# A relational graph network on one core: broadcast multiplies at the end, another order of transfers and other second norms at the start

## The chip, the core and the metric

The kernel runs on one core of a Trainium2 chip. Its engines are TensorE (PE), VectorE (DVE), ScalarE (ACT), GpSimd (POOL) and SyncE (SP), each with its own program; transfers issued by SP, ACT and POOL are moved by 16 DMA engines. The metric is the device time of one launch in microseconds (us).

## The reference

128 graphs of 128 nodes with 128 features, x; integers adj, 128x128 for each graph. With the drawn inputs adj is 0 or 1, and the code for other integers (`general`) is not entered.

```
h    = x @ W_loop.T                          # [128 graphs, 128 nodes, 128]
g    = h @ Wg_loop.T
v    = (h + b_loop) * sigmoid(g + bg_loop)
s    = x + relu(adj.T @ v)                   # first sum
x1   = (s - mean(s)) / sqrt(var(s) + 1e-5)   # first norm, over the features
m    = adj @ x1                              # messages
z    = x1 + m @ W1 + bias                    # second sum
out  = (z - mean(z)) / sqrt(var(z) + 1e-5)   # second norm
```

## The kernel before

The graphs go in 32 groups of four (GB = 4, W = 512 columns), q = 0 to 31. The host lays x, x transposed, adj and adj transposed out by group; adj and adj_t come in pairs of groups, 512 KB each. The mean of z is taken out ahead: VectorE centres the message weight and the bias (`message_weight`, `message_weight_end`, with one TensorE product L596 between), so that the second norm is only a multiply of z by 1/sqrt(var).

Each engine has a loop over t, and works on several groups with lags. TensorE at t: `loop_sum(t-1)`, `project(t)`, `message_weights(t-3)`, `messages(t-2)`; up to t = 4 (FILL) the projection comes before the loop sum, and y and messages run one group later until t = 6 (CAUGHT_UP). `project(q)` makes h and g in PSUM on top of biases that ScalarE copied there (`seed(q)`, at t = q - 2, once values(q - 2) are out). ScalarE: `copy_messages`, `norm2(t-6)` for graphs 0 and 1, `gates(t)`, `norm2` for graphs 2 and 3, `look` (counts odd integers), `seed(t+2)`. In groups 0 to 3 it also makes half of x1 (`shared_norm1`).

VectorE: `first_sum` (L930), two `bn_stats` (`first_stats`), `first_moments` (variance and mean, 128x4 each), `values(t)` (L920), `second_sum` (L990), `second_stats`. Between them it runs a chain of nine operations on 128x4 (`inverse_root`), one chain for each group from q = 0 on (FIRST_CHAIN = 5 is the t of the first), to get 1/sqrt of the second variance. `norm2(q)` waits for the chain's end.

GpSimd: for each group `norm1`: a power on 128x4 (L378), a product (L381), four multiply-adds to x1 (L387); then the issue of the next adj or adj_t transfer (L361, L368).

At the head SP issues in the order wg, w_loop_t, xt 0, raw (the integers of group 0, 256 KB, cast to floats by VectorE at L835), xt 1, x 0, xt 2, x 1, constants (192 KB), xt 3, x 2, xt 4, x 3. GpSimd issues the integers of group 1 (L415), waits for raw, issues the pair of groups 2 and 3 (`load_adj(1)`) and the transposed pair 0 and 1 (`load_adjt(0)`), waits for xt 2, issues `load_adj(2)`, and enters its loop.

At the tail the last five groups (27 = LAST to 31) get 1/sqrt from GpSimd (`last_variance` on VectorE, `last_power` on GpSimd, L409), group 31 in two halves (`half_variance2`, `half_power`, L404). Groups 30 and 31 have x1 added inside PSUM by TensorE (`inject`). ScalarE makes norm2 of 27, 28 and 30, VectorE of 29 and 31 (`last_norm2`, one multiply L1014 for each graph).

Of the kernel before, what the change touches and what calls it, by code (L numbers as in the profile page):

```python
# [47 lines left out]
FIRST_CHAIN = STAT2_LAG  # L48
# [29 lines left out]
def build(nc, x, x_t, adj, adj_t, w_in, w_loop_t, wg_loop_t, gate_bias, consts,  # L78
          w_rel_t, wg_rel_t, b_rel, bg_rel, w_msgs, rel_ids, out):
    with ExitStack() as ctx:  # L80
# [33 lines left out]
        power = sb("power", [P, GB], F32)  # L114

# [51 lines left out]
        first_adj = sem("first_adj")  # L167
        consts_in = sem("consts_in")
# [20 lines left out]
        last_power_done = sem("last_power_done")  # L189
        mean_done = sem("mean_done")  # L190
# [97 lines left out]
        def _(sp):  # L288
# [15 lines left out]
            load_xt(0)  # L304

            sp.dma_start(raw[:, :], adj[0, :, 0:W]).then_inc(raw_in, 16)  # L306
            load_xt(1)
            load_x(0)
            load_xt(2)
            load_x(1)  # L310
            sp.dma_start(const_sb[:, :], consts).then_inc(consts_in, 16)
            load_xt(3)
# [10 lines left out]
            store(LAST)  # L323
            sp.wait_ge(out_done, LAST + 2)
            store(LAST + 1)
            sp.wait_ge(out_dve, 2)
            store(LAST + 2)
            sp.wait_ge(out_done, LAST + 3)
            store(LAST + 3)
            sp.wait_ge(out_dve, 4)  # L330
# [24 lines left out]
        def _(pool):  # L355
# [50 lines left out]

            def last_power(q):
# [9 lines left out]
            pool.wait_ge(raw_in, 16)  # L417
            load_adj(1)
            load_adjt(0)
            pool.wait_ge(xt_in[2], 16)  # L420
            load_adj(2)
            pool.wait_ge(power_ready, 1)
            for t in range(GROUPS + NORM1_LAG):
# [4 lines left out]
                if t % 2 == 1:  # L428
                    load_adjt(t // 2 + 1)
                elif t > 0:  # L430
                    load_adj(t // 2 + 2)
            half_root1(0)
# [17 lines left out]
        def _(pe):  # L450
# [25 lines left out]
            def loop_sum(q):  # L476
                if exists(q):
                    spot = q // 2 % ADJ_RING * 2 + q % 2
                    if q == 0:
                        pe.wait_ge(first_adj, 1)  # L480
                    else:
# [57 lines left out]
            def messages(q):  # L539
                if exists(q):  # L540
                    spot = q // 2 % ADJ_RING * 2 + q % 2
                    pe.wait_ge(adjt_in[q // 2 % ADJ_RING], arrived(q // 2, ADJ_RING))
# [66 lines left out]
            half_messages(0)  # L609
            half_messages(1)  # L610
            half_inject(0)
# [47 lines left out]
        def _(act):  # L659
# [42 lines left out]
            def norm2(q, graphs):  # L702
                if exists(q):
                    t = q + STAT2_LAG
                    if q < LAST:
# [5 lines left out]
                    for b in graphs:  # L711
                        c = (q - LAST) * GB + b
                        r = rstd2[:, t % RSTD_RING, b:b + 1] if q < LAST else last_rstd[:, c:c + 1]
# [17 lines left out]
            def look(q):  # L731
                if exists(q):
                    spot = q // 2 % ADJ_RING
                    if q == 0:
                        act.wait_ge(first_adj, 1)
                    else:
                        act.wait_ge(adj_in[spot], arrived(q // 2, ADJ_RING))
# [81 lines left out]
        def _(dve):  # L819
# [78 lines left out]

            def last_variance(q):
# [107 lines left out]
            def last_norm2(q, graphs):  # L1007
# [3 lines left out]
                for b in graphs:  # L1011
                    c = (q - LAST) * GB + b
                    z = y_of(q, b, 1) if q in INJECTED else z_sb[:, q % Z_RING, batch(b)]
                    last = ts(out_sb[:, q % OUT_RING, batch(b)], z, last_rstd[:, c:c + 1], None, ALU.mult)  # L1014
                last.then_inc(out_dve, 1)
# [206 lines left out]
```

## Time and profile before

| what | value |
|---|---|
| median of 3 runs | 158.72 us (158.67 to 159.06) |
| the profiled execution's own time | 159.4 us |
| its span in the profile | 157.3 us |
| TensorE matmul busy | 148.7 us (95%) |
| VectorE busy | 138.4 us (88%) |
| ScalarE busy | 128.2 us (81%) |
| GpSimd busy | 113.5 us (72%) |
| moved by DMA | 42.74 MB, mean 272 GB/s |

The span is the stretch that the profile covers; the time around it (2.1 us here) is launch and end. Busy times of TensorE are modelled, since matmuls overlap. In the rows, "[idle before <-X]" is how long an engine stood and what released it; PEld is TensorE's weight load; an engine name with q is its instruction queue.

### The profile page before, as it was taken

How to read it: one execution, taken by the hardware profiler on the slowest of the kernel's cores; microseconds unless marked ns; L12 is line 12 of the kernel's file. 1: busy time of each engine (PE TensorE's matmuls, PEld its weight loads, DVE VectorE, ACT ScalarE, POOL GpSimd, SP SyncE). 2: the span in 40 equal slices, each digit the busy share in tenths (PEclk: the TensorE clock that was granted, in tenths of full speed). 3: DMA queues.
4: the chain of work that ended last, by engine and by line, in shares of the span. 5: the costliest groups of instructions: out<-in, count | busy, mean ns of one | idle time of the engine just before them, and what ended most of it. 6: DMA issues, size and time to landing. Idle time of an engine off the chain costs nothing.

```text
span 157.3 us, 3862 instructions
## 1 busy us (share of the span) xinstructions
PE 148.7 (95%) x1055; PEld 138.5 (88%) x1055; DVE 138.4 (88%) x567; ACT 128.2 (81%) x293; POOL 113.5 (72%) x221
## 2 busy tenths in 40 slices
PE   6789999999999999999999999999999999999950
PEld 3478998999999999999999999999999999999940
DVE  1329979799999999999999999999999999999962
ACT  3557997788788888998888888998888888978960
POOL 1314988865877877887777887887777886876770
PEclk9999999999999999999999999999999999999996
DMA  4899999987799899999999999998989854151144
GB/s 125 291 395 398 399 400 400 374 301 213 251 305 297 291 293 301 302 304 304 265 313 288 306 298 305 311 285 293 324 279 308 251 190 163 67 200 71 64 179 168
DMA packets 19319, 42.74 MB, mean 272 GB/s; under 512 B 2144, under 2 KB 2784, under 8 KB 19296
## 3 DMA queue, kind: packets, MB, share of 16 engines
q1 hardware_dynamic: 14400, 25.76, 48.5%
q0 software_dynamic: 4608, 16.52, 32.9%
q8 instruction: 9, 0.15, 0.4%
q10 hardware_dynamic: 288, 0.20, 0.4%
q14 instruction: 14, 0.11, 0.2%
HBM read 34.08 MB, written 8.39 MB: 270 GB/s over the span
## 4 chain that ended last, share of the span: by engine, by line
PE 84%; DVE 4%; DMA 4%; issue 3%; POOL 2%; SPq 1%; POOLq 0%; DVEq 0%
PE hg_ps L472 33%; PE loop_ps L487 18%; PE y_ps L576 16%; PE msg_ps L552 16%; DMA xt_sb<-x_t_dram 4%; POOL last_rstd L409 1%; DVE last_stats L1003 1%; POOL last_rstd L404 1%; PE aux_ps L552 1%; DVE x L973 1%; DVE s_sb L947 0%; DVE out_sb L1014 0%; DVE z_sb L990 0%; DVE stats L935 0%; SPq L306 0%
## 5 line engine op out<-in xcount | busy, mean ns | idle before, releaser
L472 PE MATMUL hg_ps<-w_all,xt_sb 128*128 128x256 f32 x256 | 60.8, 380 | 1.4 <-DMA xt_sb<-x_t_dram 1.4
L472 PEld LDWEIGHTS hg_ps<-w_all,xt_sb 128*128 128x128 f32 x256 | 46.2, 190 | 7.3 <-DMA xt_sb<-x_t_dram 1.8
L387 POOL TENSOR_SCALAR x<-s_sb,rstd,nmr 128x128 f32<-128x128 f32 x114 | 49.7, 448 | 3.3
L378 POOL TENSOR_TENSOR rstd<-var,power 128x4 f32<-128x4 f32 x31 | 32.0, 1033 | 21.0 <-DVE var L912 18.3
L715 ACT ACTIVATE out_sb<-z_sb,rstd 128x128 f32<-128x128 f32 x108 | 36.9, 392 | 0.5 <-DVE rstd L884 0.5
L673 ACT ACTIVATE hg_ps<-gate_b 128x1024 f32<-128x1024 f32 (+1 forms) x32 | 31.9, 1000 | 2.9 <-DVE vals L920 2.1
L682 ACT ACTIVATE gate<-hg_ps 128x512 f32<-128x512 f32 x32 | 19.1, 596 | 18.0 <-PE hg_ps L472 17.8
L487 PE MATMUL loop_ps<-vals,adj_sb 128*128 128x128 f32 x248 | 33.0, 276 | 0.2
L576 PEld LDWEIGHTS y_ps<-w,msg_t 128*128 128x128 f32 x240 | 31.3, 191 | 1.5
L576 PE MATMUL y_ps<-w,msg_t 128*128 128x128 f32 x240 | 31.8, 275 | 0.0
L487 PEld LDWEIGHTS loop_ps<-vals,adj_sb 128*128 128x128 f32 x248 | 30.4, 192 | 0.8 <-issue 0.5
L552 PE MATMUL msg_ps<-adjt_sb,x 128*128 128x128 f32 x232 | 30.6, 275 | 0.0
L552 PEld LDWEIGHTS msg_ps<-adjt_sb,x 128*128 128x128 f32 x232 | 28.2, 192 | 0.0
L930 DVE SCALAR_TENSOR_TENSOR s_sb<-loop_ps,x_sb 128x512 f32<-128x512 f32 x31 | 21.3, 689 | 7.3 <-PE loop_ps L487 4.0
L935 DVE BATCH_NORM_STATS2 stats<-s_sb 128x6 f32<-128x256 f32 x62 | 25.5, 427 | 0.0
L1003 DVE BATCH_NORM_STATS2 stats<-z_sb 128x6 f32<-128x256 f32 x54 | 22.8, 426 | 0.0
L740 ACT ACTIVATE seen<-adj_sb,half 128x512 bf16<-128x512 f32 x32 | 22.7, 709 | 0.0
L920 DVE TENSOR_TENSOR vals<-hg_ps,gate 128x512 f32<-128x512 f32 x32 | 21.7, 679 | 0.9 <-ACT gate L682 0.8
L990 DVE TENSOR_TENSOR z_sb<-y_ps,x 128x512 f32<-128x512 f32 x30 | 20.4, 679 | 1.1 <-PE y_ps L576 1.1
L692 ACT ACTIVATE msg_t<-msg_ps 128x512 f32<-128x512 f32 x29 | 16.8, 579 | 0.0
L361 POOL DMA_DIRECT2D adj_sb<-adj_dram x15 | 9.3, 623 | 5.5 <-DMA xt_sb<-x_t_dram 2.9
L368 POOL DMA_DIRECT2D adjt_sb<-adj_t_dram x16 | 10.1, 631 | 0.0
(93 smaller groups left out, 119.2 us busy)
## 6 DMA issues: line engine op xcount, KB each, us to landing
xt_sb<-x_t_dram SPq DMA_DIRECT2D x32, 256.0 KB, 4.3
x_sb<-x_dram SPq DMA_DIRECT2D x32, 256.0 KB, 4.3
adjt_sb<-adj_t_dram POOLq DMA_DIRECT2D x16, 512.0 KB, 4.9
out<-out_sb SPq DMA_DIRECT2D x32, 256.0 KB, 3.3
adj_sb<-adj_dram POOLq DMA_DIRECT2D x15, 512.0 KB, 5.2
raw<-adj_dram SPq DMA_DIRECT2D x1, 256.0 KB, 4.3
adj_sb<-adj_dram POOLq DMA_DIRECT2D x1, 256.0 KB, 6.6
const_sb<-consts_dram SPq DMA_DIRECT2D x1, 192.0 KB, 7.1
```

Source lines behind the costliest of these rows:

```text
L378: nc.gpsimd.tensor_tensor(r, var1[:, q % 2, :], power[:, :], ALU.pow).then_inc(rstd1_done, 1)
L387: done = nc.gpsimd.tensor_scalar(x1[:, q % X1_RING, batch(b)], s_sb[:, q % S_RING, batch(b)], r[:, b:b + 1], n[:, b:b + 1], ALU.mult, ALU.add)
L472: last = nc.tensor.matmul(hg_ps[:, q % 2, b, :], xt_sb[:, q % XT_RING, batch(b)], w_gate, start=False, stop=True, skip_group_check=True)
L487: last = nc.tensor.matmul(loop_ps[:, batch(b)], adj_sb[:, spot, batch(b)], vals[:, q % 2, batch(b)], start=True, stop=True)
L552: last = nc.tensor.matmul(msg_of(q)[:, batch(b)], x1[:, q % X1_RING, batch(b)], adjt_sb[:, spot, batch(b)], start=True, stop=True)
L576: last = nc.tensor.matmul(y_of(q, b, 1), msg_t[:, q % 2, batch(b)], w1[:, :], start=q not in INJECTED, stop=True, skip_group_check=q in IN ...
L673: nc.scalar.activation(hg_ps[:, q % 2, 0:graphs, :], gate_b[:, None, :].broadcast_to([P, graphs, 2 * P]), ACT.Copy).then_inc(seeded, 1)
L715: last = nc.scalar.activation(out_sb[:, q % OUT_RING, batch(b)], z, ACT.Copy, scale=r)
L740: nc.scalar.activation(seen[:, :], adj_sb[:, 2 * spot + q % 2, :], ACT.Square, bias=half[:, 0:1], accum_out=seen_sum[:, q:q + 1]).then_inc ...
L920: tt(vals[:, q % 2, :].rearrange("p (b n) -> p b n", b=GB), hg_ps[:, q % 2, :, 0:P], gate[:, q % 2, :].rearrange("p (b n) -> p b n", b=GB) ...
L935: got = nc.vector.bn_stats(stats[:, q % STATS_RING, p, :], s_sb[:, q % S_RING, 2 * p * P:2 * (p + 1) * P].rearrange("p (i n) -> p n i", i=2))
L1003: got = nc.vector.bn_stats(into, z.rearrange("p (i n) -> p n i", i=2))
```

## The change

- Head, SP: xt 1 goes ahead of raw, and xt 3 ahead of the constants.
- Head, GpSimd: it waits for xt 1 instead of raw, and issues the integers of groups 2 and 3 and the transposed ones of 0 and 1 as four transfers of 256 KB; group 2's and transposed group 0's have semaphores of their own. It waits for xt 3 instead of xt 2 ahead of `load_adj(2)`.
- The first half of the weight's steps on VectorE runs at t = 2 instead of t = 1.
- Second norms 0 and 1: no chains (FIRST_CHAIN = 7); VectorE writes the variance, GpSimd takes the power after norm1 and the issue of t = 5 and 6; ScalarE's norm2 waits for it.
- Tail, TensorE: half_inject(0) ahead of half_messages(1).
- Tail, VectorE: another order; half_norm1(1) after the statistics and variance of group 29; the variance of group 30 ahead of the norm of group 29; `last_norm2` is one tensor_tensor for all its graphs, with 1/sqrt as a broadcast operand: one of 128x512 from SBUF for group 29, two of 128x256 from PSUM for group 31.
- Tail, SP: store 29 ahead of store 28.

```
-FIRST_CHAIN = STAT2_LAG
+EARLY = 2
+FIRST_CHAIN = STAT2_LAG + EARLY
 ...                                                     # SP
             load_xt(0)
+            load_xt(1)
             sp.dma_start(raw[:, :], adj[0, :, 0:W]).then_inc(raw_in, 16)
-            load_xt(1)
             load_x(0)
             load_xt(2)
             load_x(1)
+            load_xt(3)
             sp.dma_start(const_sb[:, :], consts).then_inc(consts_in, 16)
-            load_xt(3)
...
             store(LAST)
+            sp.wait_ge(out_dve, 1)
+            store(LAST + 2)
             sp.wait_ge(out_done, LAST + 2)
             store(LAST + 1)
-            sp.wait_ge(out_dve, 2)
-            store(LAST + 2)
             sp.wait_ge(out_done, LAST + 3)
             store(LAST + 3)
-            sp.wait_ge(out_dve, 4)
+            sp.wait_ge(out_dve, 3)
             store(LAST + 4)
...
+            def early_power(q):
+                pool.wait_ge(early_var_done, q + 1)
+                nc.gpsimd.tensor_tensor(early_rstd[:, q, :], early_var[:, q, :], power[:, :], ALU.pow)\
+                    .then_inc(early_power_done, 1)
...
-            pool.wait_ge(raw_in, 16)
-            load_adj(1)
-            load_adjt(0)
-            pool.wait_ge(xt_in[2], 16)
+            pool.wait_ge(xt_in[1], 16)
+            pool.dma_start(adj_sb[:, 2, :], adj[1, :, 0:W]).then_inc(alone_adj, 16)
+            pool.dma_start(adjt_sb[:, 0, :], adj_t[0, :, 0:W]).then_inc(alone_adjt, 16)
+            pool.dma_start(adj_sb[:, 3, :], adj[1, :, W:2 * W]).then_inc(adj_in[1], 16)
+            pool.dma_start(adjt_sb[:, 1, :], adj_t[0, :, W:2 * W]).then_inc(adjt_in[0], 16)
+            pool.wait_ge(xt_in[3], 16)
             load_adj(2)
...
+                if 0 <= t - STAT2_LAG < EARLY:
+                    early_power(t - STAT2_LAG)
...
             half_messages(0)
+            half_inject(0)
             half_messages(1)
-            half_inject(0)
...
+                    if q < EARLY:
+                        act.wait_ge(early_power_done, q + 1)
-                    if q < LAST:
+                    elif q < LAST:
...
+            def early_variance(q):
+                dve.wait_ge(bn2_done, q + 1)
+                m2 = stats[:, q % STATS_RING, 2:4, :].rearrange("p c (i k) -> p (c i) k", k=3)[:, :, 2]
+                ts(early_var[:, q, :], m2, 1.0 / P, EPS, ALU.mult, ALU.add).then_inc(early_var_done, 1)
...
-                for b in graphs:
-                    c = (q - LAST) * GB + b
-                    z = y_of(q, b, 1) if q in INJECTED else z_sb[:, q % Z_RING, batch(b)]
-                    last = ts(out_sb[:, q % OUT_RING, batch(b)], z, last_rstd[:, c:c + 1], None, ALU.mult)
-                last.then_inc(out_dve, 1)
+                n, b = len(graphs), graphs[0]
+                c, columns = (q - LAST) * GB + b, slice(b * P, (b + n) * P)
+                z = y_of(q, b, n) if q in INJECTED else z_sb[:, q % Z_RING, columns]
+                tt(out_sb[:, q % OUT_RING, columns].rearrange("p (b n) -> p b n", b=n),
+                   z.rearrange("p (b n) -> p b n", b=n),
+                   last_rstd[:, c:c + n, None].broadcast_to([P, n, P]), ALU.mult).then_inc(out_dve, 1)
...
-                    next(steps)                             # t == CAUGHT_UP
...
-                if t == 1:
+                if t == 2:
                     weight_steps = message_weight()
                     next(weight_steps)
-                if t == 2:
                     next(weight_steps, None)
...
             half_norm1(0)
             second_stats(LAST + 2, 0)
-            half_norm1(1)
+            second_stats(LAST + 2, 1)
             dve.wait_ge(odd_count, 1)
             nc.vector.tensor_copy(flag[:, :], aux_ps[0:1, 2 * P:2 * P + 1]).then_inc(flag_ready, 1)
-            second_stats(LAST + 2, 1)
+            last_variance(LAST + 2)
+            half_norm1(1)
             second_stats(LAST + 3, 0)
-            last_variance(LAST + 2)
             second_stats(LAST + 3, 1)
-            last_norm2(LAST + 2, (0, 1))
             last_variance(LAST + 3)
+            last_norm2(LAST + 2, every)
             second_stats(LAST + 4, 0)
-            last_norm2(LAST + 2, (2, 3))
             half_variance2(0)
             second_stats(LAST + 4, 1)
```

## Rows read from the trace of the kernel before

**Rows 1.** The page: the chain's shares by engine, and GB/s in 40 slices.

```profile
GB/s 125 291 395 398 399 400 400 374 301 213 251 305 297 291 293 301 302 304 304 265 313 288 306 298 305 311 285 293 324 279 308 251 190 163 67 200 71 64 179 168
...
PE 84%; DVE 4%; DMA 4%; issue 3%; POOL 2%; SPq 1%; POOLq 0%; DVEq 0%
```

**Rows 2.** The chain of waits in order of time: start, duration, what.

```profile
2.72 5.71 DMA xt_sb<-x_t_dram
...
105.15 1.73 PE hg_ps L472 x8
106.88 0.89 PE y_ps L576 x8
```

**Rows 3.** The timeline, 5 to 12 us: start, duration, engine, line, operation.

```profile
5.13 1.97 PE L472 MATMUL hg_ps<-w_all,xt_sb 128*128 128x256 f32 x8
5.33 0.66 SPq L292 DMA_DIRECT2D xt_sb<-x_t_dram  x1
...
6.54 0.43 DVE L835 CAST adj_sb<-raw 128x512 f32<-128x512 int32 x1 [1.59 <-DMA raw<-adj_dram]
...
7.76 0.69 DVE L920 TENSOR_TENSOR vals<-hg_ps,gate 128x512 f32<-128x512 f32 x1 [0.79 <-ACT gate L682]
...
8.48 1.03 ACT L673 ACTIVATE hg_ps<-gate_b 128x1024 f32<-128x1024 f32 x1 [0.76 <-DVE vals L920]
...
10.77 0.54 POOL L361 DMA_DIRECT2D adj_sb<-adj_dram  x1 [2.87 <-DMA xt_sb<-x_t_dram]
...
11.19 1.89 PE L472 MATMUL hg_ps<-w_all,xt_sb 128*128 128x256 f32 x8
```

**Rows 4.** The timeline, 148 to 155 us.

```profile
148.28 0.58 DVE L973 TENSOR_SCALAR x<-s_sb,stats,rstd 128x128 f32<-128x128 f32 x2
...
149.74 1.01 POOL L409 TENSOR_TENSOR last_rstd<-last_var,power 128x4 f32<-128x4 f32 x1 [1.09 <-DVE last_var L904]
...
150.89 0.61 PE L530 MATMUL hg_ps<-w,msg_t 128*128 128x128 f32 x4
...
152.04 0.42 DVE L1003 BATCH_NORM_STATS2 last_stats<-hg_ps 128x6 f32<-128x256 f32 x1
152.39 1.36 POOL L404 TENSOR_TENSOR last_rstd<-last_var,power 128x2 f32<-128x2 f32 x2
...
153.12 1.27 DVE L1014 TENSOR_SCALAR out_sb<-hg_ps,last_rstd 128x128 f32<-128x128 f32 x4 [0.46 <-POOL last_rstd L404]
```

**Rows 5.** The timeline, 13 to 18 us.

```profile
13.71 1.04 POOL L378 TENSOR_TENSOR rstd<-var,power 128x4 f32<-128x4 f32 x1 [2.41 <-DVE mean_neg L914]
...
15.20 0.88 POOL L387 TENSOR_SCALAR x<-s_sb,rstd,nmr 128x128 f32<-128x128 f32 x2
...
17.05 0.68 DVE L930 SCALAR_TENSOR_TENSOR s_sb<-loop_ps,x_sb 128x512 f32<-128x512 f32 x1
...
17.70 1.89 PE L472 MATMUL hg_ps<-w_all,xt_sb 128*128 128x256 f32 x8
```

**Rows 6.** The transfer issued at 5.33 us: size, us from issue to landing.

```profile
xt_sb<-x_t_dram SPq DMA_DIRECT2D x1, 256.0 KB, 7.7
```

**Rows 7.** The timeline, 26 to 31 us.

```profile
26.77 0.97 PEld L487 LDWEIGHTS loop_ps<-vals,adj_sb 128*128 128x128 f32 x8 [0.29 <-issue]
...
29.06 0.64 POOL L368 DMA_DIRECT2D adjt_sb<-adj_t_dram  x1
29.36 0.68 ACT L715 ACTIVATE out_sb<-z_sb,rstd 128x128 f32<-128x128 f32 x2
...
30.59 0.60 ACT L682 ACTIVATE gate<-hg_ps 128x512 f32<-128x512 f32 x1 [0.55 <-PE hg_ps L472]
```

**Rows 8.** Groups by shape on VectorE from 140 us: count, busy us, mean ns.

```profile
L1014 DVE TENSOR_SCALAR out_sb<-z_sb,last_rstd 128x128 f32<-128x128 f32 x4 | 0.9, 278 | 0.8 <-POOL last_rstd L409 0.8
...
L947 DVE SCALAR_TENSOR_TENSOR s_sb<-aux_ps,x_sb 128x256 f32<-128x256 f32 x1 | 0.4, 404 | 0.0
```

**Rows 9.** The last store, issued at 154.42 us: size, us to landing.

```profile
out<-out_sb SPq DMA_DIRECT2D x1, 256.0 KB, 2.4
```

More of the change, by code:

```diff
@@ L114, in build @@
         power = sb("power", [P, GB], F32)
+        early_var = sb("early_var", [P, EARLY, GB], F32)
+        early_rstd = sb("early_rstd", [P, EARLY, GB], F32)
         w_all = sb("w_all", [P, 3 * P], F32)
@@ L167, in build @@
         first_adj = sem("first_adj")
+        alone_adj = sem("alone_adj")
+        alone_adjt = sem("alone_adjt")
         consts_in = sem("consts_in")
@@ L189, in build @@
         last_power_done = sem("last_power_done")
+        early_var_done = sem("early_var_done")
+        early_power_done = sem("early_power_done")
         mean_done = sem("mean_done")
@@ L480, in loop_sum @@
                         pe.wait_ge(first_adj, 1)
+                    elif q == 2:
+                        pe.wait_ge(alone_adj, 16)
                     else:
@@ L541, in messages @@
                     spot = q // 2 % ADJ_RING * 2 + q % 2
-                    pe.wait_ge(adjt_in[q // 2 % ADJ_RING], arrived(q // 2, ADJ_RING))
+                    if q == 0:
+                        pe.wait_ge(alone_adjt, 16)
+                    else:
+                        pe.wait_ge(adjt_in[q // 2 % ADJ_RING], arrived(q // 2, ADJ_RING))
                     await_x1(q)
@@ L712, in norm2 @@
                         c = (q - LAST) * GB + b
-                        r = rstd2[:, t % RSTD_RING, b:b + 1] if q < LAST else last_rstd[:, c:c + 1]
+                        if q < EARLY:
+                            r = early_rstd[:, q, b:b + 1]
+                        else:
+                            r = rstd2[:, t % RSTD_RING, b:b + 1] if q < LAST else last_rstd[:, c:c + 1]
                         z = y_of(q, b, 1) if q in INJECTED else z_sb[:, q % Z_RING, batch(b)]
@@ L735, in look @@
                         act.wait_ge(first_adj, 1)
+                    elif q == 2:
+                        act.wait_ge(alone_adj, 16)
                     else:
@@ L1031, in _ @@
                     next(steps, None)
+                    if 0 <= t - STAT2_LAG < EARLY:
+                        early_variance(t - STAT2_LAG)
                     if t <= FILL:
```

## The prediction

> **What bounds the kernel now.** I read the chain of waits first: its shares say that 84% of the span is TensorE [rows 1]. In order of time it is a gapless cycle of 4.4 us per group from group 8 on (1.73 us for the projections, 0.89 us each for y, message and loop sum) [rows 2], so nothing done between 40 and 140 us counts, unless it makes TensorE wait. What is left are the two ends. At the head the chain has one big DMA piece: TensorE waits for the second xt tile, issued at 2.72 us and landed at 8.43 us [rows 2]. The timeline shows the rest of the head: project(0) runs 5.13 to 7.10 us, so TensorE stands 1.4 us before project(1) [rows 3]. At the tail TensorE stops at 150.89 + 0.61 = 151.50 us, and VectorE and GpSimd work in turns until 153.12 + 1.27 = 154.39 [rows 4]; then comes the last store.
>
> **The head: xt 1 ahead of the integers.** Both transfers are 256 KB on one queue, so I let them swap landings. The integers' cast began at 6.54 us [rows 3]: xt 1 is there then, before project(0) ends, and project(1) follows at once, done by about 8.8. The integers now land at 8.43. VectorE casts them (0.43, to 8.86) ahead of values(0) in its program; the gates of group 0 are there by 7.76. values(0) takes 0.69: 9.5. loop_sum(0) starts at 9.6, where it would have been free at 8.8, and holds TensorE for 0.89: 10.46. Seed(2) on ScalarE, 1.03 us, also waits for values(0) (before 8.48, now 9.5) and ends at 10.55. xt 2 keeps its place; GpSimd's wait for it ended at 10.77 at the latest, and by the other such waits (integers: cast at 6.54, GpSimd some 0.3 later) it lands about 10.5. So project(2) starts at 10.6 instead of 11.19: lead **0.6 us** (0.4 if xt 2 is only there at 10.77) [rows 3].
>
> **Does the lead survive groups 0 to 4?** Three moves bear on it.
> (a) GpSimd now waits for xt 3, not xt 2, ahead of its loop. xt 3 was issued at 5.33 and took 7.7: 13.03 us. The 192 KB of constants no longer stand ahead of it; at 400 GB/s that is 0.5 us, so 12.5 [rows 1, 3, 6]. Add 0.3 us until GpSimd goes on and 0.54 to issue adj 2: 13.3 us. Its first power began at 13.71 (inputs now ready 0.7 earlier, 13.0), and from there to the end of x1(0) took 15.20 + 0.88 − 13.71 = 2.37 us. So x1(0) is ready at 15.7. messages(0) started at 17.70 less 0.9 for itself and 0.2 for the small product (L596) behind it, 16.6, and is wanted at 15.8 [rows 5]. No stall, with 0.1 to spare; every us that xt 3 is later than 12.6 is a us of TensorE.
> (b) The integers of graphs 4 to 7 and the transposed ones of 0 to 3 go in halves, four issues in place of two, 0.54 us each: 1.1 us more of GpSimd's queue, under the wait for xt 3, which ends later. The bytes and their order by first use are the same or better. I take nothing.
> (c) The constants land later, and the first half of the weight's steps moves from t = 1 to t = 2 on VectorE: some 0.7 us leaves one group and enters the next. The first-sum of group 2 began at 17.05 [rows 5]; it would be 0.7 earlier and is pushed back to about 17.05. values(3) is then ready at 18.3, and loop_sum(3), after project(4) (17.1 for 17.70), wants it at 18.8: hidden. The multiply for the mean waits for two of the moved steps until 16.9, which eats 0.1. Lead still 0.6.
>
> **Second norms 0 and 1 on GpSimd.** Two chains of nine 128x4 operations leave VectorE, two single ones come. TensorE stood 0.29 us at 26.8 before loop_sum(5), whose values came out of the first group with a chain [rows 7]; with about 0.5 us fewer small operations ahead of them that wait goes: **+0.3 us**, lead 0.9. The price is on GpSimd: power(0) follows x1(4) and the adjt issue. Before these end at 29.06 + 0.64 = 29.7; by now 0.7 earlier, 29.0; the power takes 1.03 (as all 128x4 ones do), so 30.1. ScalarE stands in front of norm2(0) in its program, ready at 29.36 − 0.9 = 28.5, and behind it is queued gates(6), which began at 30.59, now wanted at 29.7 [rows 7]. It comes at 30.1 + 0.7 for two norms = 30.8, done 31.4; values(6) ends at 32.1, and loop_sum(6) wants it at about 32.2. So the late gate is hidden by the wait that VectorE has for y(2) before values(6), with 0.1 us left; if that cover is gone, each later us costs one. The same again one group on, with power(1) and gates(7), where VectorE is the tighter side: I expect at most 0.1 to 0.2. ScalarE is idle for a fifth of the span, so it catches up. Head: 0.9 (from 0 to 1.3).
>
> **The tail**, in times of before. At 148.28 VectorE ran half_norm1(1), 0.58 us. Now second_stats(29, 1) runs there (0.42), then the flag and the variance of group 29, out at 148.9; the power was from 149.74 to 150.75 and is now from 149.0 to 150.0. half_norm1(1) moves 0.55 later, to 149.4; its reader, the second half of the last messages, is moved behind the injection and wants it at 149.5. Statistics and variance of group 30: 150.3; power(30) 150.34 to 151.35. TensorE's last product ends at 150.89 + 0.61 = 151.5 as before. From there: statistics 0.42, variance 0.2, power of half a group 0.69, and one multiply of 128x256 from PSUM: 151.53 + 0.42 + 0.04 + 0.16 + 0.07 + 0.69 + 0.03 = 152.94, + 0.40 (the nearest row, 128x256 out of PSUM) = 153.34 [rows 4, 8]. Before, the same end was 154.39: power(30), whose variance stood behind the first multiplies of group 29 and so behind power(29), held GpSimd until the half powers began at 152.39, and each half took two multiplies, four in 1.27 us. Gain **1.05 us**. The whole-group multiply (nearest row, a 128x512 tensor_tensor, 0.69) replaces four (0.28 each [rows 8], over 0.9 with their starts) and lies from 150.2 to 150.9, before the last halves' statistics: no part of the sum. The last store took 2.4 us [rows 9]; it now follows the one of group 30 by 0.4 us instead of 0.8, and the 256 KB ahead may cost it 0.15. Tail: **0.9** (0.4 to 1.1). The other order of stores 28 and 29 costs nothing: both are out before either of the last two.
>
> A page speaks against the broadcast multiplies. From SBUF a float32 tensor_scalar handles two elements a cycle and tensor_tensor one, with 58 fixed cycles (the Trainium skill, VectorE: DVE Perf Modes, "Why `tensor_tensor` can't do 2×_2P or 4×" and "The TRN2 errata"): as an estimate from the page, four at 0.13 us, 0.51 together, are quicker than one at 0.59. By the page the multiply costs 0.1 us more; the rows (0.28 a piece) give 0.25 less. From PSUM it gives 0.52 for two and 0.39 for one, 0.13 saved where the rows have 0.2.
>
> **Sum.** 0.9 + 0.9 = 1.8 us. The profiled execution took 159.4 with a span of 157.3; the span should be 155.5. The median of the runs is 158.72, so **156.9 us**.
>
> **Rivals.**
> 1. The forecast, 156.3 to 157.3: chance 0.55.
> 2. The head gives nothing: xt 1 shares its time with the integers instead of taking their place, or ScalarE's wait for power(0) and (1) hands the lead back at loop_sum(6) and (7). For it: margins of 0.1 us at two places. Against it: transfers on this queue landed one by one in order of issue. Tail alone: 158.72 − 0.9 = 157.8. Chance 0.17.
> 3. half_norm1(1) comes too late for the last messages, whose margin is under 0.1; the whole 0.55 by which it moved would then shift TensorE's end: tail 0.4, 157.4. Chance 0.07.
> 4. The whole-group multiply, whose two inputs both lie in SBUF, holds up power(30) beside it by its own 0.69 us: half_power(0) and (1) shift by 0.6, 157.5. Against it: GpSimd's powers took 1.01 to 1.04 us, the one beside the two-input VectorE work of the head and the one of the tail [rows 4, 5]. The rule behind it is that GpSimd's SBUF interfaces are shared with VectorE (the Trainium skill, GPSIMD Engine Reference, "Specifications"). Chance 0.06.
> 5. Slower: xt 3 lands late. In front of GpSimd's loop stands this one wait, and x1(0) hangs on it. It decides from 12.6 us on; at 14.9 us TensorE has lost 2.3 us, 0.5 more than all gains: 159.2. Against it: even with the constants ahead it landed at 13.0. Chance 0.04.
> 6. More: neither store nor gate costs anything and the stall in group 7 shrinks too: 156.3 or less. Chance 0.07. What is left (0.04) is no change at all.
>
> Range 156.2 to 158.0. Runs of this kernel differ by 0.25%, so 0.3% (0.48 us) is what can be told: faster 0.92 (cases 1 to 4 and 6), same 0.04, slower 0.04.
>
> **What would show it.** TensorE's second projection starting near 6.9 and the third at 10.6; first message sum near 15.8; no idle before loop_sum(5) and none over 0.3 at (6) and (7), with ScalarE waiting for GpSimd before norm2(0); the 4.4 us cycle unchanged; from TensorE's last product to VectorE's last multiply 1.85 us for 2.9. It is wrong if the integers land much after 8.4, if TensorE idles before messages(0), or if the last power starts more than 0.8 us after TensorE's end.

## The result: 0.67 us gained, not 1.8

| | before | after |
|---|---|---|
| median of 20 runs each | 158.88 us | 158.21 us |
| ratio, 95% interval | | 0.9957 (0.9940 to 0.9974) |
| profiled execution, its span | 159.4, 157.3 | 158.45, 156.8 |
| outside the span | 2.1 | 1.65 |

The change makes the kernel faster by 0.67 us (0.4 to 0.95 by the interval). 156.9 was forecast, and 158.21 lies above the range of 156.2 to 158.0. The direction was right; the size was nearly three times too large.

The head of the changed kernel in its chain of waits (start, duration, what), beside [rows 2] and [rows 7]:

```profile
5.69 4.07 PE hg_ps L489 x16
9.76 0.91 PE loop_ps L506 x8
10.66 1.90 PE hg_ps L489 x8
...
16.07 0.89 PE msg_ps L574 x8
16.96 0.01 issue
16.97 0.49 PE aux_ps L618 x2
17.46 1.73 PE hg_ps L489 x8
...
26.27 0.97 PE loop_ps L506 x8
```

The piece of 5.71 us for xt 1, for the last 1.38 of which TensorE stood idle, is gone: the first two projections are one piece of sixteen products. project(2) starts at 10.66, as forecast. The small product behind messages(0) takes 0.49 where it took 0.22 in the chain of before. loop_sum(5) is a piece of 0.97 with nothing in front of it.

Its timeline at the places of [rows 3] and [rows 7]: the cast of the integers, the first gate and values, GpSimd's issue of adj 2 behind the wait for xt 3; and the first early power with the norm that waits for it:

```profile
6.61 0.43 DVE L864 CAST adj_sb<-raw 128x512 f32<-128x512 int32 x1 [1.70 <-DMA raw<-adj_dram]
...
8.07 0.60 ACT L704 ACTIVATE gate<-hg_ps 128x512 f32<-128x512 f32 x1 [2.72 <-PE hg_ps L489]
...
8.70 0.69 DVE L954 TENSOR_TENSOR vals<-hg_ps,gate 128x512 f32<-128x512 f32 x1 [1.66 <-ACT gate L704]
...
10.78 0.53 POOL L369 DMA_DIRECT2D adj_sb<-adj_dram  x1 [2.39 <-DMA xt_sb<-x_t_dram]
...
29.27 1.04 POOL L417 TENSOR_TENSOR early_rstd<-early_var,power 128x4 f32<-128x4 f32 x1
...
30.34 0.69 ACT L742 ACTIVATE out_sb<-z_sb,early_rstd 128x128 f32<-128x128 f32 x2 [1.58 <-POOL early_rstd L417]
30.94 0.58 ACT L704 ACTIVATE gate<-hg_ps 128x512 f32<-128x512 f32 x1
```

Its timeline from 149 us, and the last store as SyncE's queue shows it (start, length of the issue) and in the list of transfers (size, us to landing). [Rows 4, 8, 9] have the same places of before:

```profile
149.48 0.69 DVE L1049 TENSOR_TENSOR out_sb<-z_sb,last_rstd 128x512 f32<-128x512 f32 x1
...
149.65 1.39 POOL L422 TENSOR_TENSOR last_rstd<-last_var,power 128x4 f32<-128x4 f32 x1 [0.35 <-DVE last_var L938]
...
150.21 0.61 PE L549 MATMUL hg_ps<-w,msg_t 128*128 128x128 f32 x4
...
151.01 1.35 POOL L412 TENSOR_TENSOR last_rstd<-last_var,power 128x2 f32<-128x2 f32 x2
...
152.40 0.42 DVE L1049 TENSOR_TENSOR out_sb<-hg_ps,last_rstd 128x256 f32<-128x256 f32 x1 [0.22 <-POOL last_rstd L412]
```

```profile
152.85 1.13 SPq L308 DMA_DIRECT2D out<-out_sb  x1
```

```profile
out<-out_sb SPq DMA_DIRECT2D x1, 256.0 KB, 3.5
```

TensorE ends at 150.82 and VectorE at 152.82, 2.00 us later; before it was 2.89 (151.50 and 154.39, [rows 4]). So 0.89 of the forecast 1.05 is there. But the last store took 1.13 us to issue and landed after 3.5 us, where it took 0.33 and 2.4 before [rows 9]. From VectorE's end to the end of the span it is 4.0 us, before 2.9: the span gives back 1.1.

### The profile page after: what moved, and what is told of

It reads as the page before. It is cut to its first block, busy times and chain, and to the rows that moved or that the text cites. A ratio compares the mean times of both kernels' runs of the same rounds, so it can differ in the third digit from the quotient of the medians.

```text
span 156.8 us, 3842 instructions
## 1 busy us (share of the span) xinstructions
PE 149.6 (95%) x1055; PEld 139.0 (89%) x1055; DVE 137.6 (88%) x546; ACT 127.9 (82%) x293; POOL 117.0 (75%) x225
## 4 chain that ended last, share of the span: by engine, by line
PE 88%; DVE 5%; issue 2%; POOL 1%; POOLq 0%; DVEq 0%
PE hg_ps L489 35%; PE loop_ps L506 18%; PE y_ps L598 16%; PE msg_ps L574 16%; PE hg_ps L472 1%; PE msg_ps L478 1%; DVE last_stats L1037 1%; POOL last_rstd L422 1%; DVE x L1007 1%; PE aux_ps L574 1%; POOL last_rstd L412 1%; DVE s_sb L981 0%; DVE z_sb L1024 0%; POOLq L281 0%; PE aux_ps L618 0%
## 5 line engine op out<-in xcount | busy, mean ns | idle before, releaser
L742 ACT ACTIVATE out_sb<-z_sb,rstd 128x128 f32<-128x128 f32 x100 | 34.1, 391 | 0.2 <-DVE rstd L913 0.2
L506 PE MATMUL loop_ps<-vals,adj_sb 128*128 128x128 f32 x248 | 32.9, 276 | 0.1
L369 POOL DMA_DIRECT2D adj_sb<-adj_dram x14 | 8.8, 628 | 2.4 <-DMA xt_sb<-x_t_dram 2.4
L376 POOL DMA_DIRECT2D adjt_sb<-adj_t_dram x15 | 9.6, 637 | 0.0
```

The costliest lines, as they stand in the source:

```text
L506: last = nc.tensor.matmul(loop_ps[:, batch(b)], adj_sb[:, spot, batch(b)], vals[:, q % 2, batch(b)], start=True, stop=True)
L742: last = nc.scalar.activation(out_sb[:, q % OUT_RING, batch(b)], z, ACT.Copy, scale=r)
```

## The experiments

All kernels were timed in five rounds against the kernel before on the same chip, 12 runs of each (e11: 6). "Outside" is time less span (median of the executions); the three columns behind it come from the one profiled execution: start of project(8) in the chain, VectorE's end behind TensorE's last product, end of the span behind VectorE's end; then issue and landing of the last store.

| run | time | ratio (95%) | outside | project(8) | VectorE's end | span's end | last store |
|---|---|---|---|---|---|---|---|
| e1 | 159.05 | 1.0005 (.9985, 1.0024) | 2.12 | 38.28 | 2.90 | 2.8 | 0.33, 2.3 |
| e2 | 158.2 | .9963 (.9937, .999) | 1.67 | 37.81 | 2.01 | 3.95 | 1.07, 3.4 |
| e3 | 158.72 | .9978 (.9951, 1.0006) | 1.99 | 38.34 | 2.90 | 3.1 | 0.33, 2.5 |
| e4 | 158.9 | .9985 (.9956, 1.0014) | 2.09 | 38.25 | 2.02 | 3.4 | 0.33, 2.9 |
| e5 | 158.39 | .9967 (.9944, .9989) | 1.66 | 37.42 | 2.01 | 4.0 | 1.17, 3.5 |
| e6 | 158.25 | .9971 (.995, .9992) | 1.67 | 37.42 | 2.01 | 3.8 | 1.02, 3.3 |
| e7 | 158.81 | .9992 (.9973, 1.0011) | 1.67 | 37.82 | 2.02 | 4.35 | 0.96, 3.8 |
| e8 | 158.47 | .9981 (.9957, 1.0005) | 1.66 | 38.44 | 2.00 | 4.0 | 0.33, 3.5 |
| e9 | 157.85 | .9932 (.9903, .9962) | 2.52 | 38.12 | 2.00 | 2.95 | 0.33, 2.4 |
| e10 | 158.46 | .9956 (.9917, .9995) | 2.29 | 38.30 | 2.92 | 2.5 | 0.33, 2.0 |
| e11 | 161.43 | 1.0153 (1.011, 1.0196) | 1.65 | 37.72 | 2.00 | 6.9 | 0.33, 2.4 |
| e12 | 158.57 | .9961 (.9929, .9994) | 1.67 | 37.83 | 2.01 | 4.2 | in halves |
| e13 | 158.17 | .9963 (.9941, .9985) | 2.44 | 37.77 | 2.01 | 3.5 | 0.33, 3.0 |
| e14 | 158.27 | .9958 (.9933, .9983) | 1.66 | 38.90 | 2.01 | 4.1 | 1.29, 3.6 |
| e15 | 158.22 | .9963 (.9943, .9982) | 1.79 | 37.99 | 2.01 | 3.9 | 1.06, 3.4 |
| e16 | 158.05 | .9953 (.9936, .9969) | 1.69 | 38.05 | 2.02 | 3.6 | 0.86, 3.2 |
| e17 | 158.04 | .9942 (.9919, .9966) | 1.68 | 38.28 | 1.99 | 3.9 | 1.11, 3.4 |
| e18 | 158.38 | .9981 (.9956, 1.0005) | 1.68 | 37.27 | 2.01 | 4.6 | 0.42, 4.1 |

**The two kernels again (e1, e2).** No edit.

> The kernel before, unchanged, profiled a second time: a ratio of 1.000 within its interval. Theory 1 (the last store's issue on SyncE grows from 0.33 to over 1 us when it follows the store before by 0.6 us): here the stores are 0.8 us apart, so the last issue takes 0.33 us again and the last transfer lands 2.4 us after it, the span ends 2.9 us after VectorE's last multiply. Theory 2 (such a long issue comes by chance in some executions): it can show here too. For the head: xt 0 lands 3.1 us after its issue and TensorE's first projection starts at 5.1 us if the profile before was typical.

> The changed kernel, unchanged, profiled a second time: ratio 0.994 to 0.998. Theory 1: the issue of the last store takes about 1.1 us again and the span ends some 4.0 us after VectorE's last multiply. Theory 2: 0.33 us and 2.9 us this time, and a span near 155.7. For the head: if xt 0's landing at 5.3 us (3.5 us after its issue) belongs to the new order, the first projection starts at 5.5 us again; if it was chance, at 5.1.

e1 shows what the profile of before had hidden. The start of its chain:

```profile
2.25 4.04 DMA raw<-adj_dram
6.28 0.30 issue
6.59 0.54 POOL adj_sb L361
7.12 8.59 DMA adjt_sb<-adj_t_dram
15.71 0.04 issue
15.75 1.16 PE msg_ps L552 x8
```

The same program, and no wait for xt 1 in the chain: it landed 4.2 us after its issue instead of 5.7 [rows 2], in time for project(1). What TensorE waits for here is the first transposed integers, until 15.71. project(8) starts at 38.28, in the profile of the kernel before at 38.97. The profiled execution that I worked from was 0.7 us slower at the head than three others of the same head (38.28, 38.25 in e4, 38.30 in e10). The changed head has 38.29, 37.81, 38.34, 38.44, 38.12, 37.72, 37.77, 38.90 and 37.99 in nine executions (the changed kernel, e2, e3, e8, e9, e11, e13 to e15), 38.2 in the mean.

Much of this scatter is older than anything that the change shortens: project(0) itself began anywhere between 4.99 us (e11) and 6.66 (e14, where xt 0 landed after 4.6 us). Counted from the start of project(0), project(8) comes after 32.9 us in the mean of e1, e4 and e10 (32.7 to 33.0), after 33.84 in the first profile of before, and after 32.5 in the mean of the changed head without e8 (32.2 to 32.8). By that count the head gives 0.3.

**Head alone, tail alone (e3, e4).** e3 has the last stages of before (order on VectorE and TensorE, four multiplies, order of stores) and the rest of the change; e4 the reverse:

```
--- the changed kernel
+++ e3
-            half_inject(0)
             half_messages(1)
+            half_inject(0)
...
+                for b in graphs:
+                    last = ts(out_sb[:, q % OUT_RING, batch(b)], z, last_rstd[:, c:c + 1], None, ALU.mult)
--- the changed kernel
+++ e4
-            load_xt(1)
             sp.dma_start(raw[:, :], adj[0, :, 0:W]).then_inc(raw_in, 16)
+            load_xt(1)
...
-FIRST_CHAIN = STAT2_LAG + EARLY
+FIRST_CHAIN = STAT2_LAG
```

> The changed head (order of transfers, halves, weight steps, second norms 0 and 1 on GpSimd) with the tail of before. In the two profiles TensorE's last product came 0.75 us earlier with the new head. Theory 1: the head's gain is kept in full, as the tail and its stores are those of before: 158.88 less 0.7, 158.2, ratio 0.9955, all of the measured gain. Theory 2: the gain is spread over both parts and this gets about half of it, 158.5.

> The head of before with the changed tail (order of stores, injection, VectorE's order, broadcast multiplies). VectorE's last multiply should end 0.8 us earlier, near 153.6. Theory 1: the last issue takes 1.1 us and gives all of it back: ratio 1.000, within 0.1%. Theory 2: the gain stays, 158.1, ratio 0.995.

0.35 and 0.24 us by their ratios, each with an interval that reaches 1, together 0.59 beside the 0.67 of the whole. e4 is the first sign of where the tail's gain goes: VectorE ends at 152.88 in e4 and at 153.72 in e1, 0.84 earlier with TensorE's end in the same place, yet both spans are near 156.4 and the times outside are equal.

**Single steps of the head and the store of group 30 (e5 to e8).**

```
--- the changed kernel
+++ e5
-                if t == 2:
+                if t == 1:
                     weight_steps = message_weight()
                     next(weight_steps)
+                if t == 2:
                     next(weight_steps, None)
+++ e6
-            load_xt(1)
             sp.dma_start(raw[:, :], adj[0, :, 0:W]).then_inc(raw_in, 16)
+            load_xt(1)
...
-            pool.wait_ge(xt_in[1], 16)
+            pool.wait_ge(raw_in, 16)
+++ e7
-EARLY = 2
+EARLY = 0
...
                     second_sum(t - Z_LAG - 1)
+                    next(steps)
+++ e8: store 30 leaves SyncE's queue for ScalarE's
-            sp.wait_ge(out_done, LAST + 3)
-            store(LAST + 3)
+            act.wait_ge(out_done, LAST + 3)
+            act.dma_start(out[LAST + 3], out_sb[:, (LAST + 3) % OUT_RING, :])
```

> The changed kernel, with the first half of the weight's steps on VectorE at t = 1 again. Theory A (the moved steps cost TensorE about 0.3 us: in all three profiles of the new head the mean multiply takes 0.49 us in the chain where it took 0.22, as it waits for them): the chain shows 0.22 us again, and project(4) starts 0.3 us earlier after the same project(0); in time 158.0 for 158.2, at the edge of what 12 runs tell. Theory B (the constants, which land later, are what it waits for): VectorE then stands at t = 1 until they are there, and the first sum of group 1 comes late; no gain or a loss.

> The changed kernel, with the integers of group 0 ahead of xt 1 on SyncE's queue again, and GpSimd's first wait on them. Theory A (two xt transfers in a row slow the first: xt 0 landed 3.5, 3.5 and 3.8 us after its issue with the new order, 3.0 to 3.1 with the old): xt 0 lands after 3.1 us again, project(0) starts by 0.2 us earlier, xt 1 lands after 4.2 us (before 7.0) and project(1) waits for nothing: the same time or 0.1 to 0.2 us less. Theory B (the new order is what removes the wait for xt 1 of the first profile): project(1) waits up to 1.4 us, 159.0.

> The changed kernel, with VectorE's chains for second norms 0 and 1 again and no power on GpSimd for them. Theory A (the powers remove the wait before loop_sum(5), 0.37 us in the chain, and cost nothing): the wait of 0.13 and the 1.13 us piece before and at loop_sum(5) come back, 158.5. Theory B (ScalarE's wait for GpSimd gives it back one group later): the wait before loop_sum(7), 0.30 us in the chain of before and 0.41 in the second profile of after, shrinks by as much, 158.2 as with the change.

> The changed kernel, with the store of group 30 issued by ScalarE, which makes that group's norm, instead of SyncE. Theory A (SyncE's own queue is full: its last issue took 1.13 and 1.07 us instead of 0.33 since three stores stood in it within 2 us): the last issue takes 0.33 us and the last transfer lands 2.4 to 2.8 us after it instead of 3.4; the span ends 3.0 us after VectorE's last multiply instead of 4.0, up to 1 us less, 157.4. Theory B (the DMA engines themselves are behind with the stores, whatever queue they come from): the issue is short, but the transfer still lands 3.4 us after it, and the time stays 158.2.

The product that takes 0.49 us in the changed kernel, in its timeline: TensorE waits 0.20 us for a weight step of VectorE that began at 16.63.

```profile
16.63 0.28 DVE L878 TENSOR_SCALAR const_sb<-const_sb,mid 128x128 f32<-128x128 f32 x1
...
16.97 0.30 PEld L618 LDWEIGHTS aux_ps<-const_sb,share 128*128 128x128 f32 x2 [0.20 <-DVE const_sb L878]
```

The same place in the chain of e5:

```profile
15.45 0.89 PE msg_ps L574 x8
16.34 0.22 PE aux_ps L618 x2
16.56 1.73 PE hg_ps L489 x8
```

So the weight steps, moved from t = 1 to t = 2, cost TensorE 0.27 us. The piece is 0.49 in every kernel that moves them and whose messages(0) is not late itself. The steps at t = 1 have a price of their own in some executions, in front of loop_sum(3): there e12 waits 0.10 and e16 0.08, and the piece takes 1.13 where e5, e17 and e18 have 0.89 to 0.91. In those two executions the 0.27 is lost again. e7 has the wait of before in front of loop_sum(5) back:

```profile
25.49 0.14 issue
25.63 1.13 PE loop_ps L506 x8
26.76 0.89 PE aux_ps L574 x8
```

0.14 + 1.13 against 0.97 is the 0.30 that the early norms give, and e7 is the slowest of its batch, 0.4 us over e5 and 0.55 over e6. e6 loses nothing by taking the integers first: xt 1 behind them came in time there too. Nor does the order set when xt 0 lands, as its theory A had it: 3.0 or 3.1 us after its issue with xt 1 next in e7, e8, e9, e11 and e13, and 3.7 and 3.8 with the integers next in e16 and e17. e8 shows two things. Its last issue took 0.33 us again, but the landing still took 3.5: SyncE's queue was not what was slow, what was slow lies behind it. And its chain shows my fifth rival at work, in this one execution:

```profile
4.62 8.04 DMA xt_sb<-x_t_dram
12.66 0.28 issue
...
13.58 1.06 POOL rstd L384
...
15.08 0.89 POOL x L393 x2
15.97 0.09 issue
16.06 1.02 PE msg_ps L572 x7
```

xt 3 took 8.0 us and held GpSimd, so that x1(0) came at 15.97; it cost some tenths, not 2.3 us.

**What delays the last stores (e9 to e11).** The queues named "instruction" (q8 and q14) bring the engines' own programs over the same 16 DMA engines. In the changed kernel and its share of 152 to 154 us:

```profile
q1 hardware_dynamic: 250, 0.45, 63.4%
q14 instruction: 3, 0.02, 4.9%
q8 instruction: 1, 0.02, 3.1%
```

Columns are packets, MB, and share of 16 engines; 3.1% of 16 engines over 2 us is 1.0 us of one engine, 4.9% is 1.6 us. On the page q8 has 9 packets in 0.15 MB, 16 KB each, and q14 has 14 in 0.11 MB, 8 KB each. At the end of its program each engine jumps over the code for integers other than 0 and 1. e9 and e10 leave that code out of the changed kernel and of the kernel before; e11 lets every engine wait for the last store first.

```
 # e9, e10
-            general(sp, general_pair, stores=(gout_st,), loads=general_loads)   # and the other four
 # e11
         def general(eng, steps, stores=(), loads=None):
+            eng.wait_ge(out_st[(GROUPS - 1) % OUT_RING], 16 * GROUPS // OUT_RING)
             eng.wait_ge(flag_ready, 1)
```

> The changed kernel with the code for integers other than 0 and 1 left out, so that no engine jumps over that code at its end (this part of the program is missing; what it computes for the integers at hand is unchanged). Theory A, instruction transfers for the jump over that code lie on the DMA engines beside the last stores: the last store's issue takes 0.33 us instead of 0.96 to 1.17 and it lands 2.0 to 2.6 us after it instead of 3.4 to 3.8, so that the span ends 3.0 us or less behind VectorE's last instruction instead of 3.8 to 4.35, and the span is some 1.0 to 1.3 us shorter. Theory B, four stores within 2.7 us are too many for the queue or the DMA engines: issue and landing of the last stay at about 1.0 and 3.4 us and the span ends 3.8 us or more behind VectorE.

> The kernel before with the same code left out (this part of the program is missing). Theory A: little changes at its end, since only some of the instruction transfers fell beside its last stores: its last store still takes 0.33 us to issue and 2.0 to 2.4 to land, and the span ends 2.6 to 2.9 us behind VectorE. The changed kernel without that code is then 0.9 to 1.3 us faster than this one (0.9 of the tail, 0.3 of the early norms less 0.27 of the moved weight steps). Theory B: the difference between the two stays at 0.2 to 0.7 us, as with the code in place.

> The changed kernel in which every engine waits for the last store's landing before it comes to the jump over the code for other integers. Theory A: the instruction transfers now come after the last store: its issue takes 0.33 us and it lands 2.0 to 2.6 us after it; the transfers then lie behind it, and the span may end as late as that of the changed kernel or up to 2 us later. Theory B: issue about 1.0, landing about 3.4 us as in the changed kernel.

e9's last store, on SyncE's queue and in the list of transfers:

```profile
152.69 0.33 SPq L308 DMA_DIRECT2D out<-out_sb  x1
```

```profile
out<-out_sb SPq DMA_DIRECT2D x1, 256.0 KB, 2.4
```

The last two stores are issued 0.62 us apart in e9 and e11 and 0.61 in the changed kernel, so it is not their closeness (theory B) but the instruction transfers that made the last one slow (theory A). e11 says the same with the code in place: issue 0.33, landing 2.4. There the transfers come when the engines are let go, between 155 and 158 us:

```profile
q8 instruction: 1, 0.02, 2.2%
q14 instruction: 2, 0.02, 1.3%
```

and the span ends at 159.2, 3 us later than in e2. So doing them one after the other is worse than side by side. The Trainium skill (Runtime: NRT & Kernel Launch, "Instruction fetch mechanics") says that an engine's program is brought in blocks of 16 KiB, mostly hidden, and that a taken branch whose target isn't at hand forces such a transfer. The trace agrees with the second for TensorE in the changed kernel (e9, e13); hidden it is in the middle of this kernel, not beside the last stores; and the packets are 16 KB on q8 only, 8 KB on q14.

But theory A promised 0.9 to 1.3 us between e9 and e10, and their medians differ by 0.6 (157.85 and 158.46), as with the code in place. The median span is 0.8 shorter (155.2 against 156.0), and the time outside is 0.23 longer.

**Which engine's jump (e12 to e15).** e12 is e6 and e5 together with the last store in halves; e13, e14, e15 are the changed kernel without the code on TensorE alone, on SyncE alone, on the other three.

```
 # e12, after the first of the last two multiplies
+            sp.wait_ge(out_dve, 2)
+            sp.dma_start(out[LAST + 4][:, 0:2 * P], ...)
 # e13 / e14 / e15
-            general(pe, general_pair)     # e14: sp; e15: act, pool, dve
```

> The changed kernel with the integers ahead of xt 1 again, the weight steps of the second features back at the place they had before, and the last group's store in two halves, the first sent as soon as its columns are written. By what the single edits gave, the head is 0.27 us shorter than the changed kernel's (project pieces at 0.22 instead of 0.49), and the end is unchanged or up to 0.3 us earlier if the last store's 64 KB are what lands late (theory B), unchanged if an instruction transfer holds the last packets up (theory A). 157.6 to 158.1 us beside 158.8 for the kernel before.

> The changed kernel with the code for other integers left out of TensorE's program alone (this part is missing there; nothing is changed for the integers at hand). Theory A1, TensorE's transfer of 16 packets (queue q8, 1 to 1.6 us of one DMA engine at 151 to 153) is what holds the last stores up: it is gone or comes elsewhere, the last store's issue is 0.33 us instead of about 1.0, it lands 2.0 to 2.6 us after it, and the span is some 0.8 us shorter. Theory A2, the shorter transfers of the other engines (queue q14) hold them up: issue about 1.0, landing 3.4 us as in the changed kernel.

> The changed kernel with the code for other integers left out of SyncE's program alone, the engine that issues the last stores (this part is missing there). If SyncE's own transfer held its last issue up (theory A3), issue falls to 0.33 us and landing to 2.0 to 2.6; if the transfers of other engines do (A1, A2), issue stays about 1.0 and landing 3.4 us.

> The changed kernel with the code for other integers left out of VectorE's, ScalarE's and GpSimd's programs (this part is missing there; TensorE and SyncE keep it). By theory A2 the two or three transfers of queue q14 between 152 and 154 are gone, the last issue takes 0.33 us and lands 2.0 to 2.6 us after it; by A1 nothing changes: about 1.0 and 3.4 us.

e12's halves did not help. Its two last issues on SyncE's queue:

```profile
152.16 1.57 SPq L341 DMA_DIRECT2D out<-out_sb  x1
153.77 0.64 SPq L343 DMA_DIRECT2D out<-out_sb  x1
```

e13 is the clear one of the others. (The long transfer is one packet of 16 KB, not 16 packets, as my text has it.) Its last store, then the only instruction transfer behind its span of 155.8, between 156 and 159 us:

```profile
152.33 0.33 SPq L308 DMA_DIRECT2D out<-out_sb  x1
```

```profile
q8 instruction: 1, 0.02, 2.0%
```

Without TensorE's jump the last issue is 0.33, the landing 3.0, and the median span is 155.8, 0.9 shorter than that of the kernel before in the same batch (156.7); in e14 and e15 issue and landing are those of the changed kernel. e15 against e9 is the cleanest pair: both have one short transfer beside the last store (q14), and only e15 has TensorE's 16 KB. Its last store, and the instruction transfers from 152 to 153 us:

```profile
152.55 1.06 SPq L308 DMA_DIRECT2D out<-out_sb  x1
```

```profile
q8 instruction: 1, 0.02, 6.2%
q14 instruction: 1, 0.01, 2.2%
```

So TensorE's 16 KB alone (A1) give the whole delay, 1.06 and 3.4 for 0.33 and 2.4; SyncE's own transfer (A3) is not needed for it (e14: 1.29 and 3.6). But taking the 16 KB away alone (e13, where three short ones stay) wins back the issue and only about half of the landing, 3.0. Short transfers (A2) are the likely rest: e4 has them too, its 16 KB came at 150.0, 2.9 us ahead of its last store, and that store landed after 2.9 us. How the two kinds add up no run shows. And yet the time of e13 is 158.17: the same transfer now comes behind the span, and the time outside is 2.44 instead of 1.66.

**Both mends, and TensorE's program shifted (e16 to e18).** e16 is e5 and e6 together, with whole stores. e17 and e18 add waits that are long met to it:

```
 # e17 (e18: range(5))
                     pe.wait_ge(seeded, q + 1)
+                    for _ in range(2):
+                        pe.wait_ge(weights_ready, 1)
```

> The changed kernel with the integers ahead of xt 1 again and the weight steps of the second features back where they were; early norms, the tail and whole stores stay. The pieces of the head are those of the kernel before with 0.3 us less before loop_sum(5); 157.9 to 158.3 us beside 158.8 for the kernel before if single edits add, 158.2 if the 0.27 us of the weight steps is lost in what follows.

> The kernel of e16 with two more waits that are long met in front of every projection, 64 instructions in TensorE's program and no other work. If the place of TensorE's transfers in its program decides what the end costs, they come some 4 us earlier, the one of 16 packets (q8) is gone from beside the last stores (last issue 0.33 us, landing 2.0 to 3.0 us after it), and the time outside the span stays 1.65 us: 157.2 to 157.6 us. If the jump itself calls for the transfer, it stays at 151 to 153, issue about 0.9, landing 3.2 us: 158.0 us, or more by what the waits cost TensorE.

> The same with five such waits, 160 instructions: some 10 us of the distance of 16 us between two of TensorE's transfers. By the place in the program the last stores land as in e17 or in e16, and the transfers of the stretch before come at other times; by the jump the end is that of e16. If these waits cost TensorE time (up to 0.05 us each where its queue isn't ahead), the time is up to 8 us longer.

In e17 the 16 KB transfers of the stretch before came at 120.5 and 135.5 us, where e16 has them at 124 and 141; the last stayed at 152 (151.5 in e16), with issue 1.11 and landing 3.4. So in the changed kernel the jump calls for it, not the place in the program. For the kernel before this is not shown: its last 16 KB came at 150.0 in e1 and at 150.1 in e10, which has nothing to jump over. (The trace counts 3874 instructions in e17 and 3842 in e16, 32 more for the 64 waits.) In e18 it came at 153, with one more at 149: TensorE ended at 149.79 and VectorE at 151.80, earlier than in any other kernel, and its last store landed at 155.9 all the same, after 4.1 us. Nor is the time shorter: 158.38.

Over the runs that have such a transfer near the end, it is its distance that goes with the delay. Where it began 2.3 to 3.8 us ahead of the last store's issue (before, e1, e3, e4, e10), the issue took 0.33 and the landing 2.0 to 2.9; where it began 0.2 to 1.0 us ahead (the changed kernel, e2, e5 to e8, e14 to e17), the landing took 3.2 to 3.8 and the issue, but for e8, 0.86 to 1.29. In e4 and e18, where one came at 150.0 and 149.0, an earlier store was slow to issue: 0.58 at 151.13 and 0.78 at 150.06.

## Why the prediction was wrong, step by step

**Head, xt 1 first.** project(2) at 10.6: 10.66, but for another reason. I had the integers land at 8.43; they were cast at 6.61, both transfers being there. values(0) was held by the gate of group 0, since project(0) itself began at 5.58 instead of 5.13. Parts (a) and (b): no stall, as forecast, but with a far wider margin: xt 3 landed by 10.5, where I had 12.5, and GpSimd was past it at 10.78. The exception is e8.

**Head, the lead to group 4.** Step (c), "eats 0.1", was mis-sized: 0.27 by the pieces of e5 and the changed kernel. project(4) starts at 17.46 instead of 17.1.

**Early norms.** Right: 0.30 in front of loop_sum(5), ScalarE waiting 1.58 for the power and its gate at 30.94 (forecast 30.8), with no loss at loop_sum(6). e7 supports it in the time.

**Head, the sum: the first step that failed.** Against the profiled execution the head gave 38.97 − 38.29 = 0.68, where 0.9 was forecast. But that execution was 159.4 and the median 158.72, and I took the whole gain off the median. The 1.4 us in front of project(1) belong to one slow landing: by e1, e4 and e10 project(8) starts at 38.28, by the nine executions of the changed head at 38.2. The head is worth about 0.1 in the chain, 0.3 when counted from project(0), and 0.35 in e3, whose interval holds all three. I had given the outcome "the head gives nothing" 0.17 and put it at 157.8.

**Tail, to VectorE's end.** 0.89 of 1.05. What is missing is mostly my fourth rival: power(30) beside the whole-group multiply took 1.39 instead of 1.01 and ended at 151.04, so that the two half powers stood behind it on GpSimd and the second began at 151.7, 0.13 after its variance was ready (151.50 + 0.07). The price was 0.38, not 0.69, and most of it was slack. The last power so began 0.87 us after TensorE's end, just over the 0.8 that I had named as a sign of being wrong. The rule of the Trainium skill that I had set against the rows (GPSIMD Engine Reference, "Specifications") agrees with the 1.39. The multiply itself is cheaper, as the rows had it: 0.69 for the one of 128x512, beside 0.48 and 0.46 for its four of before in two pairs.

**Tail, the last store: the second step that failed, and the larger.** "The 256 KB ahead may cost it 0.15" was 1.1 in the landing. It wasn't the 256 KB: with the same spacing e9 and e11 land in 2.4. What is new is that the last store now follows TensorE's 16 KB by 0.2 to 1.0 us instead of 2.3 or more. Part of that is the earlier store; that the 16 KB also come later in the changed kernel (151.2 to 153.1) than in e1 and e4 (150.0), though not than in the first profile of before (152.1), no run explains. And 0.45 us is found again outside the span (2.1 to 1.66), which no row of before let me see; e4, with the new tail on the old head, keeps 2.09, so it is not the tail's order alone that moves it.

**In the time.** From TensorE's last product to the end of the execution, outside included, the old tail took 7.90, 7.83 and 7.94 us (before, e1, e3), the new one 7.6 in the mean of nine executions (the changed kernel, e2, e4 to e8, e16, e17; 7.3 to 8.0). With e12 (7.9) and e18 (8.3), whose last stores or program differ more, the mean is 7.7. So 0.2 to 0.3 of the 0.89 reaches the time. With 0.1 to 0.35 from the head that is 0.3 to 0.65, beside 0.67 measured, whose interval goes down to 0.4.

**What stays open.** Why most of the tail's 0.89 does not reach the time. The late landing accounts for the span, but taking its cause away does not bring the time down as far: beside the changed kernel, e13 has a median span 0.7 shorter and the same time, e9 one 1.3 shorter and a time 0.35 shorter, with intervals that overlap. There a 16 KB transfer comes behind the span and the time outside is 2.4 to 2.5. In before, e1 and e4 an 8 KB one does (at 158, 157.5 and 157), with 2.1; in the changed kernel none, with 1.65. It looks as if the execution ends after TensorE's or another engine's last block, not after the stores; but e3 (2.0) and e10 (2.29) show no transfer there, so this is argued, not shown.

No run is clearly better than the changed kernel and complete: e17 (0.9942) and e16 (0.9953) stand beside 0.9957 with wide overlap, although both take the 0.27 out of the piece behind messages(0).

**Nothing between.** From project(8) to TensorE's end it is 112.53 us before and in the changed kernel, 112.54 in e1, 112.53 in e2: the cycle of 4.4 us is untouched, as said, and half_norm1(1), my third rival, came in time for the last messages.

## What to carry to other kernels

A wait at the head that one profiled execution shows may be that execution's alone: if its time is above the median, look for the excess in the very rows that you mean to gain from, before you subtract. At the end of a kernel an engine's gain must be followed through the stores to the end of the program: see what else uses the DMA engines there, instruction transfers too, and whether time moves outside the span. Code that is jumped over at the end isn't free: without it the kernel before takes 158.46 us, a ratio of 0.9956 (0.9917 to 0.9995), as much as the whole change gives.

## Of the hardware, what I had not expected

- One instruction transfer of 16 KB (q8, about 1 us of one DMA engine) beside the last stores goes with an issue of 1.06 us for a 256 KB store where it took 0.33, and a landing of 3.4 where it took 2.4 (e15, e9). With another queue issuing the store ahead of it the issue stays 0.33 and the landing is 3.5 (e8).
- Moved out from beside the stores it does not make the time shorter (e13: 158.17; span 155.8).
- GpSimd's 128x4 power took 1.39 us beside a 128x512 tensor_tensor of VectorE from SBUF, and 1.00 to 1.11 us otherwise, in all runs (e3 with four multiplies: 1.01 at that place).
- The same 256 KB transfer at the head lands after 4.2 or 5.7 us (xt 1, same program), and xt 3 in the new order once after 8.0.
